# A selective-scan network on one core: state sums four steps behind instead of three, projections and their evictions placed anew, and the last bf16 split kept in PSUM

## The reference, cut to what matters

```
x: (16, 8, 256, 256) float32
x = x + dilate3x3(group_norm(x))
x = x + mamba(layer_norm(unshuffle4(group_norm(x))))     # and its own residual
x = x + conv3x3(group_norm(x), w2) + b2
x = x + conv3x3(group_norm(x), w3) + b3

mamba, over 4096 tokens of 128 channels:
  x_in, z = split(u @ in_proj)                 # 256 channels each
  xc = silu(causal_conv4(x_in) + conv_b)
  dt, B, C = split(xc @ x_proj)                # 8, 32 and 32 columns
  dt = softplus(dt @ dt_proj + dt_b)
  h_t = h_(t-1) * exp(dt_t * A) + (dt_t * x_t) * B_t     # 32 states per channel
  y_t = sum over states of h_t * C_t
  y = (y + xc * D) * silu(z);  out = y @ out_proj
```

## Time and profile before

| | us |
|---|---|
| median of 3 runs | 16058.71 |
| lowest and highest | 16056.38, 16073.49 |
| the profiled execution, its own time | 16062.93 |
| its span from first to last instruction | 16061.0 |
| DVE busy | 14729.4 (92%) |
| POOL busy | 14043.5 (87%) |
| PE busy | 12586.8 (78%) |
| ACT busy | 8586.7 (53%) |

### The profile page before, as it was taken

One profiled execution on the slowest core, in us unless ns is written; L12 is line 12 of the kernel. 1 busy time (PEld: TensorE's weight loads), 2 busy tenths in 40 slices (PEclk: granted clock), 3 DMA queues, 4 the chain that ended last, 5 costly groups with the idle time before them and its releaser, 6 DMA issues.

```text
span 16061.0 us, 161052 instructions
## 1 busy us (share of the span) xinstructions
PE 12586.8 (78%) x26820; PEld 4804.5 (30%) x26820; DVE 14729.4 (92%) x13134; ACT 8586.7 (53%) x15334; POOL 14043.5 (87%) x6232
## 2 busy tenths in 40 slices
PE   4877878777787887878878787787877778778786
PEld 1333323333232332323323233232333333233232
DVE  6999999999999999999999999999999999999996
ACT  3555555555554555555555555555555555555553
POOL 5989889898898988989889898988989889898895
PEclk9999999999999999999999999999999999999998
DMA  3343333433334333343333434333343333433333
GB/s 92 103 111 106 105 112 102 118 100 102 114 102 114 99 105 112 100 114 102 105 113 102 114 102 113 105 104 112 101 118 99 102 113 101 117 99 106 111 103 84
DMA packets 1248863, 1701.30 MB, mean 106 GB/s; under 512 B 399212, under 2 KB 548148, under 8 KB 1245428
## 3 DMA queue, kind: packets, MB, share of 16 engines
q1 hardware_dynamic: 1247700, 1689.55, 37.4%
HBM read 1525.54 MB, written 124.13 MB: 103 GB/s over the span
## 4 chain that ended last, share of the span: by engine, by line
issue 36%; POOL 25%; DVE 19%; PE 9%; SPq 4%; ACT 3%; DMA 3%; POOLq 1%; DVEq 1%; ACTq 0%
POOL hc L646 16%; DVE h L1170 11%; POOL u_in L621 7%; DVE u_in L1154 5%; PE y_ps L949 5%; DMA c_sb<-bc_dram 2%; SPq L431 1%; SPq L499 1%; PE side_ps L960 1%; POOLq L643 1%; ACT a_ps L753 1%; PE side_ps L936 1%; POOL vmax L608 0%; PE proj_ps L898 0%; PE proj_ps L905 0%
## 5 line engine op out<-in xcount | busy, mean ns | idle before, releaser
L646 POOL TENSOR_TENSOR hc<-h,c_sb 128x1024 f32<-128x1024 f32 x4096 | 9889.6, 2422 | 1587.9 <-DVE h L1170 1233.5
L949 PE MATMUL y_ps<-hc,ident 128*128 128x512 f32 x16396 | 8523.0, 645 | 1519.6 <-POOL hc L646 1506.2
L753 ACT ACTIVATE a_ps<-dt,a_neg 128x512 f32<-128x512 f32 x8192 | 5619.1, 690 | 7138.8 <-DVE h L1170 7126.0
L1170 DVE TENSOR_TENSOR_SCAN h<-a_ps,carry,u_in 128x512 f32<-128x512 f32 x7168 | 8782.2, 1263 | 138.1 <-ACT a_ps L753 118.8
L949 PEld LDWEIGHTS y_ps<-hc,ident 128*128 128x128 f32 x16396 | 3159.1, 202 | 5726.5 <-issue 2900.4
L1154 DVE TENSOR_TENSOR u_in<-dtx,b_ps 128x1024 f32<-128x1024 f32 x2816 | 3375.8, 1199 | 708.7 <-PE b_ps L998 692.1
L621 POOL TENSOR_TENSOR u_in<-dtx,b_sb 128x1024 f32<-128x1024 f32 x1281 | 3046.6, 2378 | 0.1
L998 PE MATMUL b_ps<-b_parts,select 96*128 96x512 bf16 x2816 | 1113.1, 395 | 409.6 <-DVE u_in L1154 374.1
L1170 DVE TENSOR_TENSOR_SCAN h<-a_ps,u_in 128x512 f32<-128x512 f32 x1024 | 1204.5, 1204 | 71.2 <-POOL hc L646 57.1
L905 PE MATMUL proj_ps<-u_ln,w_x 128*128 128x512 f32 x2064 | 1083.3, 607 | 142.2 <-ACT xz L708 93.6
L960 PE MATMUL side_ps<-padded,w_main 128*128 128x512 f32 x1632 | 880.8, 626 | 32.6 <-ACT padded L762 17.7
(11 more groups left out here) (99 smaller groups left out, 6911.5 us busy)
## 6 DMA issues: line engine op xcount, KB each, us to landing
c_sb<-bc_dram SPq DMA_DIRECT2D x4100, 256.0 KB, 3.2
b_sb<-bc_dram SPq DMA_DIRECT2D x1283, 256.0 KB, 3.2
raw<-x SPq DMA_DIRECT2D x17, 2048.0 KB
x_dram<-vmax SPq DMA_DIRECT2D x68, 512.0 KB, 4.5
x<-x_dram SPq DMA_DIRECT2D x136, 256.0 KB, 8.3
z<-x_dram SPq DMA_DIRECT2D x68, 512.0 KB, 8.3
out<-raw SPq DMA_DIRECT2D x272, 128.0 KB
x_dram<-x SPq DMA_DIRECT2D x129, 256.0 KB, 3.9
```

Of the source, the lines that this page charges most:

```text
L646: pool.tensor_tensor(hc[:, ring_at(c * S + s, HC_RING)], h[:, ring_at(c * S + s, H_RING)], c_sb[:, s // C_GROUP % C_RING, s % C_GROUP:s % ...
L753: act.activation(a_ps[:, a_slot(c * S + s, half)], dt[:, c % 2, half], ACT.Exp, scale=a_neg[:, at:at + 1]).then_inc(a_made, 1)
L949: mm = pe.matmul(y_ps[:, half], ident[:, :], hc[:, ring_at((c * S + s) % (NC * S), HC_RING), half], start=False, stop=(s == S - 1), skip_g ...
L1170: dve.tensor_tensor_scan(h[:, r, half], a_ps[:, a_slot(c * S + s, half)], u_in[:, s % U_RING, half], start, ALU.mult, ALU.add).then_inc(h_ ...
```

## The change

It does six things.

1. `LAG` is 4: in slot s PE sums state s−4. The rings stay as they are.
2. `POOL_U` has ten states as before, at other places.
3. The tables are new. `var` is multiplied in slot 3, not 1. The `x` matmuls stand two to a slot (6, 6, 7, 7 and 9, 9, 10, 10), `z` in 12 and 14, `xproj` both in 17, `dt` in 21 and 23. ACT's evictions had stood in the slot of their last matmul; now they have slots of their own, which for `x`, `z` and `dt` are one slot number lower than that of the last matmul (6 and 9, 11 and 13, 20 and 22), and for `xproj` 16. `silus` is in 13, not 15.
4. `split_rest` writes its result over `proj_ps` in place of an SBUF tile, the middle and the low part are made from there, and `proj_ps` is free for `dt` only after `split_lo`. The parts are moved in slot 20, after `split_lo` in 19.
5. The statistics of `x1` (chunk 6) stand two to a slot in 17 to 20, not one to a slot in 15 to 22.
6. The second matmul of two group norms is one slot later (27), padding and its edge loads too.

```diff
-POOL_U = [2, 5, 8, 11, 14, 17, 20, 23, 25, 28]
+POOL_U = [2, 6, 9, 11, 14, 17, 19, 22, 25, 27]
-LAG = 3
+LAG = 4
-CENTER, VAR, OUT = 0, 1, 5
-X_AT, Z_AT = ((4, 6, 7, 8), (9, 10, 11, 12)), ((13,), (14,))
-XPROJ, DT_AT = (17, 18), ((20,), (22,))
+CENTER, VAR, OUT = 0, 3, 5
+X_AT, Z_AT = ((6, 6, 7, 7), (9, 9, 10, 10)), ((12,), (14,))
+XPROJ, DT_AT = (17, 17), ((21,), (23,))
+CENTERED, RSTD, SCALE, LAYER_NORM = 0, 2, 1, 4
+COPY_X, COPY_Z, SILU = (6, 9), (11, 13), 13
-SCALE, LAYER_NORM, BASE = VAR - 1, VAR + 2, 8
-SILU, SPLIT_REST, SPLIT_MID, SPLIT_LO, STORE_C = 15, 18, 20, 20, 19
-SPLUS_IN, SOFTPLUS, SUM_DT, DT_X, NEXT_G1 = (21, 22), 23, (23, 25), (26, 28), 30
-PLACES = ((15, 16, 19, 21), (23, 24, 25, 26), (28, 30, S + 2, S + 2))
+SPLIT_HI, SPLIT_REST, SPLIT_MID, SPLIT_LO, STORE_C, MOVE_PARTS = 16, 17, 18, 19, 18, 20
+SPLUS_IN, SOFTPLUS, SUM_DT, DT_X, NEXT_G1 = (20, 22), 23, (23, 24), (25, 27), 30
+PLACES = ((15, 16, 19, 22), (24, 25, 26, 27), (28, 30, S + 2, S + 2))
-VAR_AT = {"joint": (0, 26), "z1": (4, 0), "x1": (6, 26)}
+VAR_AT = {"joint": (0, 27), "z1": (4, 0), "x1": (6, 27)}
-PADDED_AT = ((0, 29), (4, 4))
-EDGES_AT = ((1, 1), (4, 8))
+PADDED_AT = ((0, 30), (4, 4))
+EDGES_AT = ((1, 2), (4, 8))
-RAW_STATS, Z_STATS, X1_STATS = (0, 6), (0, 14), (6, 15)
+RAW_STATS, Z_STATS, X1_STATS = (0, 6), (0, 14), (6, 17)
...
             def split_mid(b, c):
-                act.wait_ge(proj_emptied, read(b, "xproj", c))
-                act.activation(parts[:, 1, :], rest[:, :], ACT.Copy).then_inc(mid_done, 1)
+                act.wait_ge(rest_done, chunk(b, c + 1))
+                act.activation(parts[:, 1, :], proj_ps[0:S, :], ACT.Copy).then_inc(mid_done, 1)
...
-                if half == 1:
-                    act.wait_ge(lo_done, chunk(b, c + 1))
...
-            pe.sem_inc(summed, AHEAD - LAG)
...
-                dve.tensor_tensor(rest[:, :], proj_ps[0:S, :], parts[:, 0, :], ALU.subtract).then_inc(proj_emptied, 1)
+                dve.tensor_tensor(proj_ps[0:S, :], proj_ps[0:S, :], parts[:, 0, :], ALU.subtract).then_inc(rest_done, 1)
...
-                dve.tensor_tensor(parts[:, 2, :], rest[:, :], parts[:, 1, :], ALU.subtract).then_inc(lo_done, 1)
+                dve.tensor_tensor(parts[:, 2, :], proj_ps[0:S, :], parts[:, 1, :], ALU.subtract).then_inc(proj_emptied, 1)
...
-                        if c == X1_STATS[0] and 0 <= s - X1_STATS[1] < NC:
+                        if c == X1_STATS[0] and 0 <= s - X1_STATS[1] < NC // 2:
...
-                            last = x1_stats(s - X1_STATS[1])
+                            for k in range(2):
+                                last = x1_stats(2 * (s - X1_STATS[1]) + k)
```

More of the change, by code:

```diff
@@ L434, in move_parts @@
             def move_parts(b, c):
-                sp.wait_ge(lo_done, chunk(b, c + 1))
+                sp.wait_ge(proj_emptied, read(b, "xproj", c))
                 for k in range(3):
@@ L533, in _ @@
                             store_c(b, c)
-                        if s == SPLIT_LO:
+                        if s == MOVE_PARTS:
                             move_parts(b, c)
@@ L819, in _ @@
                             keep(b, *behind(c, s, 1))
-                        if s == CENTER:
+                        if s == CENTERED:
                             centered(b, c)
-                        if s == VAR:
+                        if s == RSTD:
                             token_rstd(b, c)
@@ L826, in _ @@
                         for half in range(NH):
-                            if s == X_AT[half][-1]:
+                            if s == COPY_X[half]:
                                 copy_x(b, c, half)
-                            if s == Z_AT[half][-1]:
+                            if s == COPY_Z[half]:
                                 copy_z(b, c, half)
@@ L834, in _ @@
                             silus(b, c)
-                        if s == XPROJ[-1]:
+                        if s == SPLIT_HI:
                             split_hi(b, c)
```

7 lines of the change are left out of this document (3 added, 4 removed).

## The result

The changed kernel takes **15,625.92 us** (median, 15,612.70 to 15,632.34) against 16,057.54 for the kernel before in the same comparison: a ratio of **0.9731, 95% interval 0.9716 to 0.9747**. The forecast was 15,400, range 15,250 to 15,780. It went the way I said and inside the range, but 432 us came where I had said 659. The profiled executions say the same, 16,061.0 against 15,620.4 us of span. Medians in this document are of the fast executions: one of the four of the kernel with the convolution's old slots took 30,314 us, and with it that kernel's median would be 15,578.67, 47 us under the changed kernel instead of 65.

What follows compares the result with a forecast made beforehand. DVE, busy 92%, was taken as the bound, its idle time mostly waits for PE's queue. Gains of 954 us less costs 90, 154, 32 and 15 gave 663 us off, so 15,400 us, range 15,250 to 15,780.

Steps and rivals of the forecast that it cites:

- (a): Chunk 6: with the patches' wait gone, DVE waits 5.6 us for `hc` of 14, 16 times: 90 us lost.
- (b): Chunks 1 to 4: POOL's `hc` late at states 22 and 27, 2.4 us in each of 64 chunks: 154 us lost.
- (c): Image border: the first scan waits for `hc` of the last state, 2 us more, 16 times: 32 us lost.
- (d): Scans waiting for ACT's decays, which silus and evictions hold up: no gain, 15 us charged.
- Part 1: Low part of B on DVE: `split_lo`, now reading PSUM, takes 0.679 us instead of 2.079, saving 181 us.
- Part 2: PE's spread of B no longer queued behind what waits for POOL or ACT: 643 us saved, gate's wait 26 more.
- Part 3: DVE's own waits: the split's for ACT's high part, 31 us, and the `x1` statistics' for patches, 73 us, go.
- POOL takes over: Rival, chance 0.13: every wait for the spread becomes one for `hc`, the 643 us don't come, giving 15,763.
- POOL behind PE: Rival, chance 0.05: `hc` waits for a sum moved behind PE's spread, so POOL binds the kernel, slower at 16,240.
- ACT held up: Rival, chance 0.06: ACT's evictions wait for PE with decays queued behind them, costing 294 us, giving 15,690.
- no effect on the spread: Rival, chance 0.03: PE is late from too much work, so half of the 643 us stays, giving 15,720.
- The signs: Expected profile: `split_lo` 679 to 690 ns, `b_ps` wait under 150 us, `hc` wait 300 to 450, POOL busy 91% or more.

Runs made afterwards that it cites:

- the kernel with the three pieces: Changed kernel with the old POOL slots of `u`, convolution's second group in slots 23 to 26, and output stores one slot earlier: 15,442.55 us, ratio 0.9625.
- the convolution's piece: Changed kernel with only the second group of convolution matmuls one slot earlier, 23 to 26 in place of 24 to 27: 15,561.09 us, ratio 0.9698.

## Why the prediction was right or wrong, point by point

| term | forecast us | measured us |
|---|---|---|
| split, busy time of DVE | −181 | 355.7 to 169.6: −186 |
| DVE's wait for `b_ps` | −643 | −576 |
| gate | −26 | −21 |
| split's wait for ACT | −31 | −32 |
| `x1` statistics | −73 | −74 |
| wait for `hc`: (a), (b), (c) | +276 | +371 |
| ACT's decay (d) | +15 | +15 |
| dilation's steps, busy time | none | +98 |
| other small groups, starts and ends | none | −36 |
| sum | −663 | −441 |

**What bounds the kernel.** Right: DVE's idle time was what there was to win, PE's queue held it, and POOL was next.

**Part 1, the split.** Right, and for the reason given. The 680 of a low part that had not waited was its price, and the kernel with the rest in SBUF turns the 2.7 us on again. Of the two bounds on the write into PSUM, 0 was right: the rest takes 661 ns, not more than the 679 into SBUF. Against the estimate from the Trainium skill, "VectorE: DVE Perf Modes", "The TRN2 errata — SBUF-src ops pay a fixed extra latency per instruction", the form that reads PSUM is not 65 ns dearer here: 653 against 680.

**Part 2, the spread.** The mechanism was right, `dt` and the slow sum with it, and the size 67 us off, by two errors against each other. The border's 49 that I kept are gone. In their place stand 62 us in slot 28, 21 in slot 6 and 21 in slots 22 and 23. The first is what the new places of the convolution do: PE's wait for an addition in the slot before, 1.0 to 1.5 us in each of chunks 1, 2 and 4 and 0.3 in chunk 5. I had gone through ACT and POOL for what stands ahead of a spread, and not through DVE itself. The gate's 26 was right in size; the kernel with the lag alone shows that 319 us hang on `var` being moved. The slow sum is gone from behind the `dt` matmuls, but not from the kernel: of about 4,100 sums 458 took over 2.2 us before and 668 do now, and PE's granted clock fell from 0.933 to 0.916 (the last section says what goes ahead of a slow sum). No term had that.

**Part 3.** Right by name, as was the remark that the 73 us come back in (a). The kernel with the statistics back in slot 15 makes it firm: worth nothing.

**(a) to (d).** Chunk 6 came as computed, 5.5 us in each image, 88 against 90. Chunks 1 to 4: slot 22 has 1.7 to 1.9 where I had 1.0, slot 27 only 0 to 1.3 where I had 1.6, together 136 against 154. **The border (c) is the term that failed**: 163 us in place of 57, so +106 where I had +32. I took POOL's own work as what is late there. It is also the C rows, queued on SP behind the output rows: the change issues these a slot later, behind POOL's input for state 27 and one more of its products, and POOL's stop at the end of chunk 7 grew from 4.2 to 7.0 us, which is 44 us in 16 images. In the kernel with the three pieces, where the stores start as early as before, DVE waits 98 us in the last state and at the border where it had waited 66: that is the 32 that (c) had, though other things differ in that kernel as well. The working had named that queue in chunk 6 and did not look at it at the border. Another 41 us of waits for `hc` stand at places for which I had none, the most in slot 7 of chunk 0 (20) and in slot 14 of chunks 5 to 7, where my margin was under 0.7 us. ACT (d) came out as said in its total, and that is luck: behind the silus stand 86 us, and nothing in chunks 1 to 4 where I had 0.5 in each, while 56 us stand in other slots where I had 15.

**What no step had**: the dilation. Its two-input steps on DVE grew by 98 us (the last section says why). The prediction had read "waiting inside the instruction" off the low part and not asked which other instructions have both inputs in SBUF.

**The rivals.** *POOL takes over* is what happened in part, by its mechanism, the ring of three, at some places and not everywhere; the wait for `hc` was between the forecast's 342 and that rival's. *POOL behind PE*, *ACT held up* and *no effect on the spread* did not come: POOL waits 149.3 us for sums where it waited 128.3 (within an image 57 where it was 10), ACT's evictions wait for PE (305.0 for those of `x`), but they are covered, and the decay costs DVE 142.6.

**The signs.** Two of them missed by little: POOL is busy 90% and not 91, as the whole is longer than forecast, and `split_lo` reads 652 to 678 ns, under the 679 to 690.

Which of the three pieces shorten the stop at the end of chunk 7 can be read from when the stores start: by that it takes the slots of `u` and the stores together, and the convolution's piece moves nothing there (6.5 us with it alone, as in after). What these two alone would give in time is open, as no kernel had only them.

## What to carry to other kernels

When PE's order is loosened so that a queue no longer holds up the busiest engine, look at whoever has slack of a few per cent (POOL here, 40 us in an image of 979): its short stops turn into waits against the ring between the two, and a buffer more was worth 155 us here, nearly as much as the split (172). Look up every stop of that engine before, and what is queued ahead of the small transfers that it needs, not only its total. Ask of a ring whether the number of its uses in a loop is a multiple of its depth. A lag in the order of sums and the table that fills the slots are one change: the lag alone cost 1.2%, the new table without it 6.7%.
